# Turning the two parts of the input by transposing DMA instead of TensorE in a projection stage

## The reference

```python
q = jnp.einsum('bsd,ed->bse', x, Wq).reshape(bsz, seqlen, HQ, D)   # HQ = 32 heads, D = 128
k = jnp.einsum('bsd,ed->bse', x, Wk).reshape(bsz, seqlen, HK, D)   # HK = 8
v = jnp.einsum('bsd,ed->bse', x, Wv).reshape(bsz, seqlen, HK, D)
q = _rope(_rmsnorm(q, q_norm_w), pos)
k = _rope(_rmsnorm(k, k_norm_w), pos)
...
o = jnp.einsum('bhqk,bkhd->bqhd', probs, v_all)     # probs: masked softmax of q against cache and new keys
x = x + jnp.einsum('bse,de->bsd', o.reshape(bsz, seqlen, HQ * D), Wo)
```

## Time and profile before

| | us |
|---|---|
| median of 3 runs | 2235.04 |
| lowest and highest | 2233.54 and 2237.6 |
| the profiled execution, whole | 2237.23 |
| its span from first to last instruction | 2235.3 |
| busy in the span: PE / DVE / ACT / POOL | 2079.8 / 1690.8 / 1478.1 / 1099.7 |
| mean granted TensorE clock, as a share of full speed | 0.982 |

### The profile page before, as it was taken

One profiled execution on the slowest core, in us unless ns is written; L12 is line 12 of the kernel. 1 busy time (PEld: TensorE's weight loads), 2 busy tenths in 40 slices (PEclk: granted clock), 3 DMA queues, 4 the chain that ended last, 5 costly groups with the idle time before them and its releaser, 6 DMA issues.

```text
span 2235.3 us, 56731 instructions
## 1 busy us (share of the span) xinstructions
PE 2079.8 (93%) x17328; PEld 1357.1 (61%) x17328; DVE 1690.8 (76%) x4445; ACT 1478.1 (66%) x4201; POOL 1099.7 (49%) x1841
## 2 busy tenths in 40 slices
PE   0886999999999986899999999999999999999999
PEld 0443454555555444677777777777777777777775
DVE  7787677777777766777777777777777777777774
ACT  0443676777777665677777777777777777777774
POOL 3343455555555554454454454554554544544542
PEclk9998999999999998999999999999999999999999
DMA  7886355655556658988888888888888888788881
GB/s 288 291 292 240 119 192 179 195 197 197 195 191 230 203 187 300 293 251 249 253 249 245 260 248 250 250 249 250 253 245 253 253 242 259 246 249 254 248 246 63
DMA packets 402134, 522.58 MB, mean 234 GB/s; under 512 B 50867, under 2 KB 297523, under 8 KB 399796
## 3 DMA queue, kind: packets, MB, share of 16 engines
q1 hardware_dynamic: 361012, 371.71, 52.6%
q0 software_dynamic: 40832, 147.34, 20.4%
HBM read 426.36 MB, written 92.54 MB: 232 GB/s over the span
## 4 chain that ended last, share of the span: by engine, by line
PE 54%; SPq 3%; DVE 3%; DMA 1%; issue 1%; ACT 0%; DVEq 0%; POOL 0%; POOLq 0%; ACTq 0%
PE att_scores L1497 14%; PE att_y L1545 14%; PE att_tr L1506 10%; PE att_o L1533 5%; PE att_o L1535 4%; PE att_o L1534 4%; SPq L102 1%; SPq L96 1%; PE att_tr_new L1512 1%; PE att_o L1536 1%; DVE att_prob L1644 1%; PE att_scores L1498 1%; DVE att_mask L1630 1%; DMA att_keys<-k_parts 1%; DVE att_tpl L1668 0%
## 5 line engine op out<-in xcount | busy, mean ns | idle before, releaser
L1644 DVE CUSTOM_DVE_ANT_0 att_prob<-att_scores,att_mask 128x544 f32<-128x544 f32 x512 | 371.0, 725 | 296.5 <-PE att_scores L1498 292.7
L1576 ACT ACTIVATE att_tph<-att_tr 128x512 f16<-128x512 f32 x512 | 306.3, 598 | 334.9 <-PE att_tr L1506 333.5
L1443 POOL CAST att_parts<-att_norm 128x96 f16<-128x96 f32 x512 | 135.1, 264 | 567.1 <-issue 557.8
L1545 PE MATMUL att_y<-att_wo,att_ot 128*128 128x512 f16 x1536 | 407.5, 379 | 0.0
L1668 DVE TENSOR_TENSOR att_tpl<-att_tr,att_tph 128x512 f16<-128x512 f32 x512 | 350.3, 684 | 0.8 <-ACT att_tph L1576 0.5
L1506 PE MATMUL att_tr<-ident,att_norm 128*128 128x128 f32 x2048 | 327.4, 283 | 0.0
L1109 POOL TENSOR_TENSOR proj_rn<-proj_ra,proj_rb 128x512 f32<-128x512 f32 x128 | 190.4, 1488 | 242.1 <-DVE proj_rb L1234 242.1
L983 PE MATMUL proj_blk<-wh,proj_xt 128*128 128x512 f16 x768 | 293.3, 382 | 0.8 <-DVE proj_xt L1190 0.8
L984 PE MATMUL proj_blk<-wl,proj_xt 128*128 128x512 f16 x768 | 293.5, 382 | 0.0
L985 PE MATMUL proj_blk<-wh,proj_xt 128*128 128x512 f16 x768 | 293.3, 382 | 0.0
L1533 PE MATMUL att_o<-att_tph,att_values 128*128 128x128 f16 x1536 | 284.8, 220 | 6.0 <-DMA att_values<-v_parts,att_idx 3.8
(11 more groups left out here) (196 smaller groups left out, 4875.2 us busy)
## 6 DMA issues: line engine op xcount, KB each, us to landing
room<-k_parts SPq DMA_DIRECT2D x512, 128.0 KB, 2.6
att_keys<-k_parts SPq DMA_DIRECT2D x512, 128.0 KB
q_parts<-proj_turned SPq DMA_DIRECT2D x128, 256.0 KB, 3.4
v_new_parts<-proj_vp SPq DMA_DIRECT2D x64, 256.0 KB, 3.7
room<-q_parts SPq DMA_DIRECT2D x32, 512.0 KB, 6.7
att_query<-q_parts SPq DMA_DIRECT2D x32, 512.0 KB
pro_ring<-in_w_t SPq DMA_DIRECT2D x12, 1024.0 KB, 7.3
room<-in_w_t POOLq DMA_DIRECT2D x24, 512.0 KB, 5.9
```

Of the source, the lines that this page charges most:

```text
L1545: last = mm(y_ps[:, :], ot[p][:, a, h, :], wo[:, h, w, :], start=(h == 0 and start), stop=(h == HQ - 1 and stop))
L1576: copy = lambda out, in_, **kw: nc.scalar.activation(out, in_, ACT.Copy, **kw)
L1644: v.tensor_tensor_reduce(out=prob[q][:, :], in0=sc[q], in1=mask[bi % 2][:, at:at + LK], scale=1.0, scalar=-3.0e38, op0=ALU.add, op1=ALU.ma ...
```

## The change

The PSUM tensor `xp`, PE's eight transposes per tile and DVE's copy are gone. In their place SP issues two transposing transfers per tile, one for `xh` and one for `xl`, each from a 128x512 fp16 buffer into its half of `xt` (128x4x128). For tile 0 they stand ahead of all other transfers of SP's list except the two loads of x. For tile t+1 they stand in step 8 of tile t, behind the store of the heads of block 4. They wait for `xhigh` and `xlow` of the tile, and for all blocks of the tile before the current one. PE begins a tile when `xturned` says that both have landed; ACT and DVE wait on the same count before they write `xh` and `xl` anew. The cut diff:

```diff
-        xp = ctx.enter_context(nc.psum_tensor("proj_xp", [P, 2 * D], F16))
...
+            def turn_x(t, p):
+
+                sp.wait_ge(xhigh, t + 1)
+                sp.wait_ge(xlow, t + 1)
+                after(sp, blk_done, (t - 1) * BLK)
+                for h, part in enumerate((xh, xl)):
+                    sp.dma_start(xt[p][:, :, h, :], part[:, :], transpose=True).then_inc(xturned, 16)
+
+            turn_x(0, 0)
             for c in range(2):
                 load_chunk(0, c)
...
+                    if n == 8 and not is_tile(t, NT - 1):
+                        turn_x(t + 1, 1 - p)
...
-            def turn_x(t, p):
-
-                pe.wait_ge(xhigh, t + 1)
-                pe.wait_ge(xlow, t + 1)
-                after(pe, xt_done, t)
-                for k in range(KD):
-                    for h, part in enumerate((xh, xl)):
-                        at = (2 * k + h) * P
-                        last = nc.tensor.transpose(xp[:, at:at + P], part[:, k * P:(k + 1) * P], ident16[:, :])
-                last.then_inc(xturned, 1)
...
-                pe.wait_ge(xt_done, t + 1)
+                pe.wait_ge(xturned, 2 * 16 * (t + 1))
...
-                    if n == ROT - 1 and not is_tile(t, NT - 1):
-                        turn_x(t + 1, 1 - p)
...
-            def keep_xt(t, p):
-                dve.wait_ge(xturned, t + 1)
-                v.tensor_copy(xt[p][:, :, :, :].rearrange("p k h c -> p (k h c)"), xp[:, :]).then_inc(xt_done, 1)
...
-                        if n == ROT:
-                            keep_xt(t + 1, 1 - p)
```

More of the change, by code:

```diff
@@ L734, in projections @@
         tq = [ctx.enter_context(nc.psum_tensor(f"proj_tq{i}", [P, D], F32)) for i in range(2)]
-        xp = ctx.enter_context(nc.psum_tensor("proj_xp", [P, 2 * D], F16))
         xin = [sem(f"xin{i}") for i in range(2)]
-        xchain, scaled, xhigh, xlow, xturned, xt_done = (sem(s) for s in (
-            "xchain", "x_scaled", "x_high", "x_low", "x_turned", "xt"))
+        xchain, scaled, xhigh, xlow, xturned = (sem(s) for s in (
+            "xchain", "x_scaled", "x_high", "x_low", "x_turned"))
         blk_done, rot_done, sq_done, v_read = (sem(s) for s in ("block", "products", "squares", "v_block_read"))
@@ L988, in body @@
                         turn_heads(*heads_at(t, n))
-                    if n == ROT - 1 and not is_tile(t, NT - 1):
-                        turn_x(t + 1, 1 - p)
-            turn_x(0, 0)
             tiles(pe, body)
@@ L1002, in x_high @@
                 act.wait_ge(scaled, t + 1)
-                after(act, xturned, t)
+                after(act, xturned, 2 * 16 * t)
                 copy(xh[:, :], x3[p][:, :], scale=col[p][:, 2:3]).then_inc(xhigh, 1)
@@ L1183, in x_low @@
                 dve.wait_ge(xhigh, t + 1)
-                after(dve, xturned, t)
+                after(dve, xturned, 2 * 16 * t)
                 v.scalar_tensor_tensor(out=xl[:, :], in0=x3[p][:, :], scalar=col[p][:, 2:3], in1=xh[:, :],
                                        op0=ALU.mult, op1=ALU.subtract).then_inc(xlow, 1)
-            def keep_xt(t, p):
-                dve.wait_ge(xturned, t + 1)
-                v.tensor_copy(xt[p][:, :, :, :].rearrange("p k h c -> p (k h c)"), xp[:, :]).then_inc(xt_done, 1)
             def mean(t, p):
@@ L1271, in _ @@
             x_low(0, 0)
-            keep_xt(0, 0)
             tiles(dve, body)
```

## The result

The changed kernel takes 2277.9 us in the median of 4 runs (2276.3 to 2282.9), the kernel before 2236.3 in the runs beside it. The ratio is 1.0186 with a 95% interval of 1.016 to 1.0213: slower by 41.6 us. The profiled execution took 2278.6 us, with a span of 2276.7, 41.4 above the span before.

What follows compares the result with a forecast made beforehand. The landing of the value stores plus 4.30 us of fixed work was taken to set PE's pace. Later landing 33.6, clock falls 22.1, start 3.1, tile 0 -0.45 summed to +58.3 us, 2293 us forecast, range 2250 to 2345.

Steps and rivals of the forecast that it cites:

- The mechanism: Projection tiles: value stores land later behind the transposing transfers, PE goes on 4.30 us after ACT's release, and its clock falls.
- X: Time the two transposing transfers on SP add to the landing of the value stores: 2.4 us per tile, 14 tiles, 33.6.
- Removed work gains nothing: PE's turns (0.45 us per tile) and DVE's copy, projection stage: removal only lengthens waits, gain zero except in tile 0.
- The 0.45 us in tile 0: Only tile 0 keeps the gain of PE's removed turns, as its chain does not begin with a store: -0.45 us.
- The middle between bytes and number: Choice of X from the value stores' 1.6 us apiece: 1.6 by bytes, 3.2 by number, so 2.4 us.
- the sign given beforehand: SP's timeline: if the two new issues take far more than 0.5 us each, X is SP's time, not the queue's.
- its bounds of 1.0 and 5.2: Ends of X: 1.0 us with issuing and moving side by side, 2274 us; 5.2 with transfers one after another, 2332.
- The clock: PE's matmuls after the longer wait run at the 1.2 GHz level in all 14 tiles, 13 new falls of 1.7 us: 22.1.
- the rival in which it does not fall: PE's clock stays up after the longer waits: 2252, 2271 and 2310 us for X of 1.0, 2.4 and 5.2; chance 0.17.
- The start: Tile 0, from xl to the first matmul: two issues and two landings, 5.0 us instead of 1.94, +3.1 us.
- The rival of piece by piece: Transposing transfers handle eight 128x128 pieces one after another: X 13.6, 2460 us, or 10.5, about 2415 us; chance 0.11.
- The rivals of hidden transfers and of a gain: Value stores land unchanged, X 0, 2236 to 2238 us, chance 0.06; or the chain moves up 0.45 us, 2228, chance 0.03.

Runs made afterwards that it cites:

- The experiment with one turn: The kernel before with one of TensorE's eight turns of x in tiles 1 to 15, DVE's copy kept: 2241.9 us, ratio 1.0022.
- the stores moved: Value stores in SP's step 7: in the kernel before, instead of step 9, 2222.5 us; in the changed kernel, behind the transposing transfers also moved there, 2222.5 us.
- eight small transfers: The kernel before plus eight 2.5 KB transfers to a scratch tensor, issued by SP where the change puts its two: 2322.2 us, ratio 1.0386.
- the plain pair: The kernel before plus two plain 128 KB transfers of xh and xl at the place of the transposing ones: 2270.0 us, ratio 1.0132.

## Why the prediction came out as it did

**The mechanism** held in each of its links, that of the clock in 9 of 14 tiles. The value stores behind the transposing transfers land later, PE's wait follows ACT's at 4.30 us, and the time of 2277.9 lies between the 2274 worked out for X = 1.0 and the forecast of 2293.

**Removed work gains nothing**: right. PE's 0.45 us per tile went into its wait; ACT's wait was 3.1 us per tile, inside the 2.6 to 6.8 said beforehand. The experiment with one turn, and the 6.0 us that appear only with the stores moved, show it from both sides. The 0.45 us in tile 0 did not show either: that stretch took 41.33 us against 41.32. Two more matmuls at its beginning run on the low clock.

**X** was one of two terms that were mis-sized: 1.5 us, not 2.4. The middle between bytes and number was the wrong way to choose. Each half of the reasoning had an error, and they partly cancelled: SP's time per issue is 1.28 us and not 0.46, but the stores' own time from issue to landing is not a constant to which a delay is added. It was 6.2 us in the mean with 0.73 MB still queued ahead of them, and fell to 4.8 with 0.28 MB; whether that is the reason stays open. By the sign given beforehand, issues far over 0.5 us each, X is SP's time and not the queue's; one step earlier and with eight small transfers SP's time was what counted. That X fell inside its bounds of 1.0 and 5.2 is therefore partly luck: neither bound was reckoned from what happened. 14 x 0.9 is 12.6 us too much.

**The clock** was right in kind. The falls cost 1.7 us each as read from the earlier trace rows, so the rival in which it does not fall is out, but only 9 of the 14 waits brought one, not all: waits of 2.47, 2.59, 2.70 and 2.81 us passed without, others of 2.47, 2.51, 2.57 and 2.70 did not. That is 8 new falls behind this wait (7 in the 14 tiles of the table, one in the last tile) in place of 13, 8.5 us too much. In the kernel with the plain pair a wait of 2.90 us passed without and one of 2.03 did not. A fall is no function of the length of the wait alone; what else decides it these runs don't show.

**The start** was 2.1 us longer, 3.1 forecast. The errors of 12.6, 8.5 and 1.0 are in part offset by 4.7 us that no term held, 2.7 in earlier stages and 2.0 in the attention, and by the 0.45 of tile 0 that did not come; together they make the 17 us between the forecast span and the measured one. The 4.7 is scatter between executions as far as the traces tell, and so luck.

**The rival of piece by piece** is out. Landing of the transposing transfers, by the list of transfers from 240 to 830 us:

```profile
proj_xt<-proj_xh SPq DMA_TRANSPOSE x15, 3.5
proj_xt<-proj_xl SPq DMA_TRANSPOSE x15, 2.6
```

The second lands after 2.6 us, as a plain one of 128 KB elsewhere, and PE never waits for `xt` behind tile 0. The closest comparison is the plain pair in the same place:

```profile
proj_xt<-proj_xh SPq DMA_DIRECT2D x15, 128.0 KB, 3.3
proj_xt<-proj_xl SPq DMA_DIRECT2D x15, 128.0 KB, 3.3
```

From the first issue to the landing of both it is 3.9 us for the transposing pair and 4.0 for the plain one, in the median of 15 tiles. By the rule of the Trainium skill in "Advanced Engine Details and Errata", X-Bar Transpose, a transposing transfer is as fast as a regular one; this case agrees as far as landing goes. The hold of the issuing engine is another matter: 1.28 us for one, where the plain pair took 0.61 to 0.73 each. The Trainium skill's 1309 ns for a 128x128 piece in "VectorE: DVE Perf Modes", The three transpose paths, cannot be scaled by the number of pieces: four of them took 1.28 us of SP and 2.6 us to landing.

**The rivals of hidden transfers and of a gain** are out at the place of the change. One step earlier the transfers are hidden, but by SP's idle time and not by an emptier queue.

## What to carry to other kernels

Before asking what an operation costs on its new engine, ask what stands behind it in that engine's list, and whether somebody waits for it. The same two transfers cost 42 us ahead of the value stores; one step earlier, where SP waited anyway, they cost about 3 us, with an interval that holds zero. Work removed from the busiest engine is worth nothing while a wait of that engine, however small (1.0 us per tile here), is ended by something else; find what ends it, and move that first.

## What the runs showed of the hardware

- A transposing transfer of 128x512 fp16 held SP for 1.24 to 1.32 us in the changed kernel, and for 1.21 to 3.00 us (median 1.26) when it was issued one step earlier; a plain one of the same bytes took 0.61 to 0.73 in the place of the change, and one of 2.5 KB about 0.48.
- The time from the first issue to landing of four stores of 1 MB together lay between 4.4 and 7.4 us in the kernels before and after the change, 6.19 in the mean with 0.73 MB queued ahead of them and 4.82 with 0.28 MB. A delay of their issue by 2.8 us was half made up so. Behind three transfers of 2.5 KB, with 0.30 MB queued, they took 5.65.
- Idle TensorE costs twice: after waits of 2.5 to 4.0 us the clock was granted at half for about 3.4 us, 9 times of 14, and a kernel with 1.94 us of useless matmuls per tile in the same wait was 8 us faster in the median, with overlapping intervals.
